# Placing the 48 row-maximum products of an attention step by a table, in uneven numbers a unit

## What is computed

```
q, k, v = x Wq', x Wk', x Wv'          (rotary embedding on q and k)
s = q k' / 4 + bias(i - j)             (bias within a band of 256, causal)
m = max(max_j s, offset)               (one maximum per row and head)
p = exp(s - m);  o = p v / (sum p + exp(offset - m))
x = layernorm(x + o Wo')
x = layernorm(x + linear(mxfp4(x), mxfp4(W)) + b)
```

## Time and profile before

| what | value |
|---|---|
| median of 3 runs | 1636.56 us (1636.11 to 1637.26) |
| the profiled execution, its own time | 1639.82 us |
| the profiled execution, its span | 1637.9 us |
| PE busy / DVE busy / ACT busy in the span | 1550.1 / 1289.1 / 1112.0 us |
| granted TensorE clock, mean | 0.983 of full speed |
| start of the first exponential of step 0, step 1, step 2 | 305.3, 344.8, 379.2 us |

### The profile page before, as it was taken

One profiled execution on the slowest core, in us unless ns is written; L12 is line 12 of the kernel. 1 busy time (PEld: TensorE's weight loads), 2 busy tenths in 40 slices (PEclk: granted clock), 3 DMA queues, 4 the chain that ended last, 5 costly groups with the idle time before them and its releaser, 6 DMA issues. The chain is left out here.

```text
span 1637.9 us, 28803 instructions
## 1 busy us (share of the span) xinstructions
PE 1550.1 (95%) x9542; PEld 810.6 (49%) x9552; DVE 1289.1 (79%) x3828; ACT 1112.0 (68%) x1620; POOL 257.3 (16%) x159
## 2 busy tenths in 40 slices
PE   8999999899999999999999999999999998899974
PEld 6877677444444444444444444444444443344431
DVE  5668988788888888888888887888888876289995
ACT  5543444587877887878878788887788788434542
POOL 6545454300000000000000000000000000033432
PEclk9999999999999999999999999999999999999985
DMA  5695757453335434344333543433443302013221
GB/s 199 195 250 178 193 176 197 132 94 57 47 58 105 62 47 83 51 74 86 65 47 47 106 72 47 80 52 60 73 93 47 47 15 79 26 52 103 78 77 51
DMA packets 129257, 147.59 MB, mean 90 GB/s; under 512 B 48595, under 2 KB 81427, under 8 KB 129110
## 3 DMA queue, kind: packets, MB, share of 16 engines
q1 hardware_dynamic: 129110, 145.76, 40.2%
HBM read 102.32 MB, written 42.60 MB: 88 GB/s over the span
## 5 line engine op out<-in xcount | busy, mean ns | idle before, releaser
L1050 ACT ACTIVATE probs<-ps 128x1024 f32<-128x1024 f32 (+3 forms) x768 | 595.3, 809 | 178.5 <-PE ps L743 118.1
L1320 DVE CUSTOM_DVE_ANT_0 junk<-ps,bias_q 128x384 bf16<-128x384 f32 (+2 forms) x1024 | 503.0, 503 | 147.3 <-PE ps L716 133.7
L716 PE MATMUL ps<-k_stack,q_stack 96*128 96x384 bf16 (+3 forms) x1536 | 492.5, 334 | 14.5 <-DVE mx L1320 4.6
L737 PE MATMUL ps<-q_stack,k_stack 99*128 99x512 bf16 (+3 forms) x1536 | 491.7, 328 | 12.5 <-ACT ps L1065 4.9
L1313 DVE TENSOR_REDUCE mx<-ps 128x1 f32<-128x128 f32 (+3 forms) x768 | 365.3, 485 | 45.7 <-PE ps L716 38.7
L743 PE MATMUL ps<-bias_r,ident_r 128*128 128x384 f32 (+2 forms) x1280 | 352.1, 363 | 0.0
L716 PEld LDWEIGHTS ps<-k_stack,q_stack 96*128 96x128 bf16 x1536 | 142.6, 97 | 366.9 <-DVE mx L1320 152.8
L758 PE MATMUL ps<-probs,v_sb 128*17 128x512 f32 (+3 forms) x3072 | 322.8, 492 | 0.1
L808 PE MATMUL ps<-split 128*128 128x512 f32 x1152 | 285.6, 406 | 9.7 <-POOL split L1202 7.0
L808 PEld LDWEIGHTS ps<-split 128*128 128x128 f32 x1152 | 216.7, 191 | 52.2 <-POOL split L1202 7.9
L743 PEld LDWEIGHTS ps<-bias_r,ident_r 128*128 128x128 f32 x1280 | 222.5, 193 | 36.8
(11 more groups left out here) (124 smaller groups left out, 1101.7 us busy)
## 6 DMA issues: line engine op xcount, KB each, us to landing
q_stack<-q_parts SPq DMA_DIRECT2D x192, 128.0 KB, 4.3
k_stack<-k_parts SPq DMA_DIRECT2D x32, 384.0 KB, 7.3
q_parts<-q_stack SPq DMA_DIRECT2D x84, 128.0 KB, 2.1
k_parts<-k_stack SPq DMA_DIRECT2D x84, 128.0 KB, 2.0
v_dram<-v_sb SPq DMA_DIRECT2D x32, 272.0 KB, 2.7
v_sb<-v_dram SPq DMA_DIRECT2D x32, 272.0 KB, 9.0
k_stack<-k_parts SPq DMA_DIRECT2D x32, 256.0 KB, 8.0
q_stack<-h SPq DMA_DIRECT2D x16, 512.0 KB, 4.1
```

What stands on the lines that cost most here:

```text
L716: pe.matmul(ps_ring[:, use.bank, 0:c1 - c0], q_stack[0:STACK, b, hl, I * P:(I + 1) * P], k_stack[0:STACK, b, hl, c0:c1], start=True, stop= ...
L737: mm = pe.matmul(ps_s[:, u % 2, hh, 0:w], k_stack[0:ROWS, b, hl, J * P:(J + 1) * P], q_stack[0:ROWS, b, hl, i0:i0 + w], start=not in_bank, ...
L1050: act.activation(probs[:, (u // 2) % 3, 2 * pr:2 * pr + 2, 0:w], ps_s[:, pr, :, 0:w], ACT.Exp).then_inc(exp_done, 1)
L1320: ins = dve.tensor_tensor_reduce(out=junk[:, use.bank, 0:c1 - lo], in0=ps_ring[:, use.bank, lo - c0:c1 - c0], in1=bias_q[:, hl, BAND - t0 ...
```

## The change

`units_beside` takes the number of products inside and behind each unit from a table. The order of the 48 products, the units, and the places of M, O1, O0 and `shifts` stay as they are. The table gives up to two inside and up to three behind; u22 and u23 get none, as before.

```
--- before.py
+++ after.py
@@ -102,11 +102,23 @@
 SPREAD = 22
 
 
+
+
+MAXIMA_OF_UNIT = (
+    (2, 1), (1, 1), (2, 0), (0, 2), (2, 0), (1, 1),
+    (1, 0), (1, 1), (0, 1), (2, 1), (0, 3), (0, 1),
+    (2, 3), (0, 1), (1, 2), (1, 1), (2, 0), (1, 2),
+    (1, 1), (2, 0), (1, 0), (0, 3), (0, 0), (0, 0),
+)
+assert len(MAXIMA_OF_UNIT) == NU and sum(map(sum, MAXIMA_OF_UNIT)) == NM
+assert not any(map(sum, MAXIMA_OF_UNIT[SPREAD:]))
+
+
 def units_beside(u):
 
-    ks = list(range(min(NM, NM * u // SPREAD), min(NM, NM * (u + 1) // SPREAD)))
-    return ks[:1], ks[1:]
-
+    done = sum(map(sum, MAXIMA_OF_UNIT[:u]))
+    inner, behind = MAXIMA_OF_UNIT[u]
+    return list(range(done, done + inner)), list(range(done + inner, done + inner + behind))
 
 
 PV_LEFT, EVAC_LEFT, OT_LEFT = 1, 1, 4
```

## The result

| | before | changed |
|---|---|---|
| median | 1637.40 us (1636.11 to 1639.51, 7 runs) | 1643.54 us (1641.23 to 1645.70, 7 runs) |
| profiled execution: its own time, span | 1639.82, 1637.9 us | 1645.70, 1643.7 us |
| a step in the middle (distance of u0's exponentials) | 34.44 us | 34.60 us |

The ratio is 1.0034, 95% interval 1.0024 to 1.0043: slower by 0.34%, beyond the 0.2% that I took as no change. My likeliest case was 1639.3 us and "same"; the time lies within the range, and "slower" had a chance of 0.36. Of the 4.2 us between the likeliest case and the measured median, 1.8 arise in the steps (4.5 instead of 2.7) and 1.3 behind them; 0.8 is the median before, which is 1637.40 us in these runs and was 1636.56 in the three that the forecast started from.

A forecast was written before the change was run, and what follows sets the result against it. PE was taken to set the step. New waits of 1.45 us against 1.39, taken as 0.08 a step, gave 2.4 us over thirty steps; with 0.3 in step 0, 1636.56 + 2.7 = 1639.3 us, range 1631 to 1645.5.

The forecast's parts named there:

- the tenth, O1: O1, after u4's products: it waits 0.03 us for the bank that k8 used.
- likeliest case: Whole kernel: 2.7 us slower, 1639.3 us; forecast's chance 0.45, and the outcome "same" 0.46.
- the 1.39 us a step: PE's seven old waits in a step: 0.60 us for ACT's bias, 0.79 for a ring bank; all the edit could win.
- stalls are moved, not removed: Whole step: ring waits 0.79 become 1.12 us, ACT's 0.60 become 0.33; no change to about +0.15 a step; chance 0.45.
- the ten places: The places in a step where PE would newly wait, 1.45 us together against 1.39 before.
- The two-part maximum's turnaround: Products with a 128-column reduction ahead of the fused maximum: bank held 1.33 us, giving waits of 0.17 at k18, 0.29 in u12.
- k14's 0.05: k14, moved into u7: it waits 0.05 us for k11, whose reading DVE begins late, after O1's outputs.
- k32 and k43: Last product behind u14 waits 0.11 us for O0's bank; second inside u19 waits 0.08 for k40's.
- The 0.3 us of step 0: Step 0: k4 now lies ahead of M, and M needs k2's read instead of k1's, costing another 0.3 us.
- The faster one: Rival: two-part maximum turns its bank round in 1.15 us, so -0.38 a step, 1625 us; sign changes from 1.29 down; chance 0.08.
- The slower one: Rival: ACT's copies come late at u17, u19 and u21; if by 0.25, some 0.4 us a step, 1651 us; chance 0.08.
- the spacing of 131 ns: Rival: 512-column matmuls 131 ns apart, not 0.22 us; 0.27 us a step, 8 us in all, slower; chance 0.02.

The follow-up runs named there:

- the best tables: Two new tables for the whole step, made by the turnaround rule, against the kernel before: 1609.26 and 1607.70 us, ratios 0.9823 and 0.9819.
- e11: Changed kernel with ScalarE copying the old outputs ahead of the bias for u3, not behind it: 1647.81 us, ratio 1.0061 to the kernel before.
- e4: Changed kernel with one product, k1, behind u0 and not inside it: 1640.58 us, ratio 1.0014 to the kernel before.
- e2: Only u6 to u16 follow the new table, the rest placed evenly as before: 1635.16 us, ratio 0.9976 to the kernel before.
- e3: Only u17 to u21 follow the new table, the rest placed evenly as before: 1640.94 us, ratio 1.0016 to the kernel before.
- e7: Another table for u0 to u5, u6 to u16 as in the changed kernel, u17 on evenly as before: 1620.50 us, ratio 0.9893 to the kernel before.
- e10: Changed kernel with k28 behind u13 and not behind u12: 1640.07 us, ratio 1.0016 to the kernel before.
- The eleven runs above: The follow-up kernels: nine differ from the changed kernel in the table alone, one leaves out a reduction, one moves a copy; 1607.70 to 1647.81 us.
- e8_no128: Changed kernel without the plain 128-column reductions ahead of the fused maximum in products 3 and 11 of each head: 1638.00 us, ratio 0.9998 to the kernel before.

## Why the prediction was right or wrong

- **What bounds the kernel** held. PE sets the step, an edit of places can only move its waits, and nothing went past the 1.39 us a step that I counted as the most there is to win: the best tables win 1.0.
- **That stalls are moved, not removed** held, and nine of the ten places were within 0.08 us and the tenth, O1, within 0.09. The direction of the sum was right; the size, 0.08 us a step, was measured as 0.15, at the very end of the forecast's own range. That it came even so near is in part luck: the terms below are off by some 0.3 us upwards and 0.2 downwards.
- **The terms that were mis-sized**, or put at nothing:
  - (1) No wait was counted before u3's product with v: 0.09. I had counted that k6, which lay inside u3, is done ahead of it, but not that PE then comes 0.17 sooner to the product with v. That product needs the copy of the old outputs, which ends as far behind u3's first product as before: 726.49 + 0.58 - 726.70 = 0.37 us, and 729.01 - 728.64 = 0.37. Before, PE was there 727.29 - 726.70 = 0.59 behind u3's first product, late enough; now it would be there after 0.42, and starts at 0.51, 0.14 behind the copy. e11 shows that it is the copy. The shift of ScalarE's chain by k1 inside u0 is not the reason: e4 takes it away and has the same 0.51, and e2 and e3, with a product inside u3, have no such wait.
  - (2) O1: 0.12 instead of 0.03, and the transposes take 732.44 - 731.98 = 0.46 us where e7's, without a wait, take 720.67 - 720.23 = 0.44. The bank was free when I said: k8's reduction ends at 731.15 + 0.69 = 731.84, and at a product's pace, 0.06 behind that, O1 would have waited 0.04. But its first weight load starts only at 731.95, 0.11 behind the read, and the first transpose 0.03 behind its load. In the kernel's code the transposes wait for two semaphores, so the ring's wait is an instruction of its own, and their weights are of 4 bytes; that the one costs the later load and the other the 0.03 is read from the rows and was not tried.
  - (3) The two-part maximum's turnaround is 1.25, not 1.33: k15 starts at 735.47, and k18, the second of two at 736.46, at 736.46 + 0.17 + 0.09 = 736.72. I had added 0.20 to a turnaround of a fused product, but the reduction starts earlier than the fused operation would. This took 0.08 off k18 and 0.08 off u12.
  - (4) k14's 0.05 didn't come.
  - (5) k32 and k43 took 0.02 more each and k10 and k22 0.01 each, and the last units cost 0.03 beside k43's wait (e3: 0.13 less 0.10), of which 0.02 were in the forecast's few hundredths.
  - The sum 0.09 + 0.09 + 0.02 - 0.08 - 0.08 - 0.05 + 0.02 + 0.02 + 0.02 + 0.01 is 0.06, of the 0.07 missed.
- **The 0.3 us of step 0** is in the rows but not shown in the time. M's weight load comes 5.31 us behind the step's first exponential, and came 4.93 behind it. The step grew from 39.49 to 39.92 us, 0.43, of which 0.15 is any step's, so this pair of executions agrees. But e10, whose table is the same up to u11 and whose M comes at 5.31 us too, has a step 0 of 39.25 us. A stretch at 1.2 GHz lies in step 0 of all three, alike in these two (mean clocks of 0.52 and 0.63 over 308 to 312 and 312 to 316 us before, 0.53 and 0.61 after) and otherwise in e10 (0.57 and 1.00); a step 0 in one execution can't tell 0.3 us.
- **What I left out** was the stretch behind the steps: 1.3 us in the profiled execution, with a longer half clock at the head of stage three. Whether the edit causes it is open. The eleven runs above all have the same code there. In their profiled executions the half clock at that place is as long as the changed kernel's in six (265.3 to 265.4 us behind step 31's start), as short as before's in two (264.2 and 264.5) and absent in three (262.2 to 262.6).
- **The rivals.** The faster one rested on a two-part turnaround under 1.29. It is 1.25, and the kernel was slower all the same, since misses (1), (2) and (5) outweighed it. The slower one (copies late at u17, u19, u21) didn't occur: no wait before these units. Nor did the spacing of 131 ns that the Trainium skill gives (TensorE: Matmul & The Clock Gate, Back-to-back issue gap) show: products of 512 columns stay 0.22 us apart.

## What to carry to other kernels

Where one engine, working through a fixed order, sets the time and shares a small ring with a slower reader, count for each use the turnaround (product, wait, read, release) and the work that the first engine has until it needs that bank again; a placement is good when no such work is shorter than the turnaround and when the products stand where another wait would be. "Few at the busy spots" is not the measure: three products of 512, 384 and 512 columns in a row cost 0.16 us behind u10 and nothing behind u3 (e7). When work is taken out of a place, list everything that the engine now reaches sooner and what each of these waits for, not only the wait that is there today. And two new waits in one place may be one backlog: test parts of a change alone before adding up stretches of the whole.

## What was not expected of the hardware

A fused maximum that finds VectorE idle starts 0.53 us after its 384-column product began, of which the product itself takes 0.34; a plain reduction of 128 columns in a product of 512 starts 0.42 us after it (735.47 to the row below), 0.03 us behind the product's end. Of the changed kernel, DVE's timeline:

```profile
735.89 0.29 DVE L1325 TENSOR_REDUCE mx<-ps 128x1 f32<-128x128 f32 x1 [0.22 <-PE ps L728]
...
736.57 0.08 DVE L1332 DVE_READ_ACCUMULATOR2_ANT mx<- 128x1 f32 x1
```

Its accumulator is read by 736.57 + 0.08 = 736.65, and k18, which takes that bank, follows.

In e8_no128 the fused operation of such a product has no instruction ahead of it and carries the wait itself. PE's row of the product and DVE's of the fused operation:

```profile
737.21 0.39 PE L728 MATMUL ps<-k_stack,q_stack 96*128 96x512 bf16 x1
```

```profile
737.63 0.56 DVE L1332 CUSTOM_DVE_ANT_0 junk<-ps,bias_q 128x384 bf16<-128x384 f32 x1 [0.53 <-PE ps L728]
```

It too starts 0.42 us after its product, 0.03 us behind the product's end (737.21 + 0.39). The fused operations that have a semaphore instruction of their own in between (`dve_passed`) start later: the one of the earlier trace rows 0.53 us after its product, which is 0.53 - 0.34 = 0.19 us behind the product's end, so 0.16 us more. That this instruction costs the 0.16 us was not tried by itself.
